# Ranking twelve batches of tokens one stage earlier in a fused attention and mixture-of-experts kernel

## What is computed

```
y   = LN(attention(LN(x)))            # 16 heads of 64, one shared k/v head, causal,
                                      # learned relative-position bias, one null key
out = x + shared(y) + sum over the 2 best of 7 experts of w_e * expert_e(y)
expert(h) = (silu(h @ g.T) * (h @ u.T)) @ d.T      # 128 -> 352 -> 128
w = the two best softmax(y @ wr.T + rb), scaled to sum to 1
```

## Time and profile before

| what | value |
|---|---|
| three timed runs | 437.86, 432.62, 437.17 us; median 437.17 |
| the profiled execution: its own time | 437.97 us |
| the profiled execution: span, first to last instruction | 436.2 us |
| TensorE (PE) busy | 359.3 us, 82% |
| VectorE (DVE) busy | 291.2 us, 67% |
| ScalarE (ACT) busy | 279.5 us, 64% |
| GpSimd (POOL) busy | 228.7 us, 52% |
| mean granted TensorE clock | 0.923 of full speed |

### The profile page before, as it was taken

One profiled execution on the slowest core, in us unless ns is written; L12 is line 12 of the kernel. 1 busy time (PEld: TensorE's weight loads), 2 busy tenths in 40 slices (PEclk: granted clock), 3 DMA queues, 4 the chain that ended last, 5 costly groups with the idle time before them and its releaser, 6 DMA issues. The chain is left out here.

```text
span 436.2 us, 10247 instructions
## 1 busy us (share of the span) xinstructions
PE 359.3 (82%) x2921; PEld 297.6 (68%) x2922; DVE 291.2 (67%) x1144; ACT 279.5 (64%) x935; POOL 228.7 (52%) x253
## 2 busy tenths in 40 slices
PE   0286776999999999999997989587948999999930
PEld 0275655677777777777775647487948999899920
DVE  2838385888888898888889893568524555555514
ACT  1374684999999999999996783345523444444410
POOL 5024833688766667667772542076750444444430
PEclk9997995999999999999999687859997999999995
DMA  6726199970000000000000000011111222121118
GB/s 187 198 78 198 52 221 207 207 141 2 2 2 2 3 2 2 3 0 2 2 2 2 1 2 0 2 50 51 55 43 45 57 61 61 49 60 58 39 19 271
DMA packets 39479, 26.54 MB, mean 61 GB/s; under 512 B 4465, under 2 KB 37131, under 8 KB 39439
## 3 DMA queue, kind: packets, MB, share of 16 engines
q1 hardware_dynamic: 33680, 19.55, 20.1%
q0 software_dynamic: 2240, 4.23, 2.9%
q10 hardware_dynamic: 3518, 2.26, 1.8%
HBM read 12.89 MB, written 13.54 MB: 61 GB/s over the span
## 5 line engine op out<-in xcount | busy, mean ns | idle before, releaser
L675 ACT ACTIVATE p_space<-p_space,low 128x129 f32<-128x129 f32 x256 | 99.0, 392 | 6.3 <-DVE low L1011 6.3
L494 POOL TENSOR_TENSOR p_space<-p_space,inv 128x516 f32<-128x516 f32 x64 | 67.0, 1049 | 66.1 <-DVE inv L1019 66.1
L1007 DVE SCALAR_TENSOR_TENSOR p_space<-bank,rn,biasm_space 128x129 f32<-128x129 f32 x256 | 72.1, 344 | 22.2 <-PE bank L1181 21.9
L485 POOL TENSOR_TENSOR biasm_space<-bias,madd 128x516 f32<-128x516 f32 x64 | 75.6, 1193 | 7.4 <-DVE p_space L1007 7.3
L536 POOL DMA_INDIRECT result_rows<-oT_space,dest_ring x38 | 37.3, 982 | 60.3 <-DVE dest_ring L1147 60.3
L760 ACT ACTIVATE biasm_space<-bank 128x384 f32<-128x384 f32 x54 | 26.6, 492 | 58.3 <-PE bank L1178 58.2
L1178 PE MATMUL bank<-ident,p_space 128*128 128x128 f32 (+1 forms) x272 | 48.5, 297 | 2.4 <-POOL p_space L494 2.1
L675 ACT ACTIVATION_READ_ACCUMULATOR p_space<-p_space,low 128x1 f32 x256 | 48.6, 190 | 0.0
L1181 PE MATMUL bank<-DT,biasm_space 128*128 (+1 forms) x324 | 46.5, 281 | 1.3 <-ACT biasm_space L760 1.3
L1181 PE MATMUL bank<-GH,yh 128*128 (+1 forms) x108 | 41.3, 382 | 6.8 <-DVE yl L1118 6.8
L690 ACT ACTIVATE pT<-bank 128x512 f32<-128x512 f32 x64 | 37.3, 583 | 13.7 <-PE bank L1181 12.5
(11 more groups left out here) (217 smaller groups left out, 682.8 us busy)
## 6 DMA issues: line engine op xcount, KB each, us to landing
sent_rows<-fill_row SPq DMA_DIRECT2D x2, 1950.0 KB, 23.0
sent_rows<-fill_row SPq DMA_DIRECT2D x2, 1885.0 KB, 19.1
q_space<-sent_rows SPq DMA_DIRECT2D x38, 65.0 KB
xs<-in_x_dram SPq DMA_DIRECT2D x4, 256.0 KB, 6.4
bias<-bias_rows SPq DMA_DIRECT2D x1, 1024.0 KB, 6.0
xnT<-result_rows ACTq DMA_DIRECT2D x4, 256.0 KB, 6.1
xn<-result_rows SPq DMA_DIRECT2D x4, 256.0 KB, 5.2
out_dram<-xs SPq DMA_DIRECT2D x4, 256.0 KB, 2.4
```

The lines of the kernel that those rows point to most:

```text
L485: nc.gpsimd.tensor_tensor(biasm[:, b % 2, heads, :], bias[:, heads, :], madd[:, b:b + 1, :].to_broadcast([P, HC, KEYS]), ALU.add).then_inc ...
L494: nc.gpsimd.tensor_tensor(v, v, spread(inv[:, b % 2, heads], KEYS), ALU.mult).then_inc(p_normed, 1)
L675: last = nc.scalar.activation(v, v, ACT.Exp, bias=low[:, b % 2, h:h + 1], accum_out=den[:, b % 2, h:h + 1])
L1007: last = nc.vector.scalar_tensor_tensor(Pb[:, q, h, :], src, rn[:, q, h:h + 1], biasm[:, q, h, :], ALU.mult, ALU.add)
```

## The change

- `choose(0)` is followed at once, in step 18, by `mark(0)`, `rank(0)` and `share_out(0)` on VectorE, all ahead of `keep_y` of batch 15. `count(0)` stands at the head of step 18 on TensorE, ahead of `mix(3, 3)`, and `weigh(0)` at the head of step 18 on ScalarE, ahead of `keep_oT(1, 3)`.
- `count(0)` writes into `bank[3]` instead of `bank[6]`, and waits for the copy of the transposed y that was in `bank[3]`.
- A send no longer waits for shared tiles.
- Tiles 8 to 15 are written out instead of looped. `AHEAD = 16` takes the place of `NB` in the order of tiles; the order itself stays the same.
- Both halves of the results are read by SyncE, eight DMAs, the two halves of a group one after the other. The second half goes into the space of `bias` instead of `xnT`.

```diff
+    AHEAD = 16
+    LAPS = (ROUTED - RING) // RING
...
+        shared_rows = bias[:, :, :].rearrange("p a b -> p (a b)")[:, 0:NB * D].rearrange("p (b d) -> p b d", d=D)
...
-        result_in = (xn, xnT[:, :].rearrange("p (b d) -> p b d", b=NB))
+        result_in = (xn, shared_rows)
...
+        def count_bank(k):
+            return (3, 6)[k]
...
             for u in range(2 * RING):
                 single(u)
                 between(u)
-            with eng.Fori(0, NB // RING - 2) as i:
-                for m in range(RING):
-                    step(RING * i + (2 * RING + m), m, i + 2, lambda k: "shared")
-            for u in range(NB, NB + RING):
+            for u in range(2 * RING, AHEAD + RING):
                 single(u)
...
-        def load_results(eng, k):
+        def load_results(eng):
...
             for g in range(NB // 4):
-                eng.dma_start(result_in[k][:, 4 * g:4 * g + 4, :],
...
+                for k in range(TOP):
+                    eng.dma_start(result_in[k][:, 4 * g:4 * g + 4, :],
...
                     for b in batches:
-                        need(pool, down_kept, min((TOP * batches.start + n * len(batches) + b - batches.start - 8) // 2, NB - 3))
                         nc.gpsimd.indirect_dma_start(
...
                 if t == NB + 1:
                     exp(3, 2)
+                if t == NB + 2:
+                    weigh(0)
                 keep_q(0)
                 keep_pT(0)
...
             nc.scalar.activation(send[0][1][:, :, 0:D], y_sb[:, 0:Y_FIRST, :], ACT.Copy).then_inc(send_made[0][1], 1)
-            weigh(0)
...
             run_tiles(act, step, between)
-            load_results(act, 1)
...
                 if t == NB + 2:
                     choose(0)
+                    mark(0)
+                    rank(0)
+                    share_out(0)
                 keep_y()
...
-            mark(0)
-            rank(0)
-            share_out(0)
             own(nc.vector.memset(h_sb[:, :, I:ICH * IC], 0.0))
...
+                if k == 0:
+                    pe.wait_ge(yT_kept, y_bank.index(count_bank(0)) + 1)
+                mm(bank[count_bank(k)][:, 2 * k * P:2 * k * P + n * NE], before[:, :], load_flat, True, True)
...
+                if t == NB + 2:
+                    count(0)
                 queries(0)
                 turn_p(0)
                 mix(3, 3)
...
             pe.wait_ge(oT_kept, 2 * NB)
-            count(0)
```

More of the change, by code:

```diff
@@ L296, in run_tiles, with kind_of @@
         def run_tiles(eng, step, between):
+            def kind_of(n):
+                return None if not 0 <= n < TILES else "routed" if AHEAD <= n < AHEAD + ROUTED else "shared"
             def single(u):
-                step(u, u % RING, u // RING, lambda k: None if not 0 <= u - k < TILES else
-                     "shared" if u - k < NB else "routed")
+                step(u, u % RING, u // RING, lambda k: kind_of(u - k))
             for u in range(2 * RING):
@@ L312, in run_tiles, with batch_of @@
                 for m in range(RING):
-                    step(RING * i + (NB + RING + m), m, i + (NB // RING + 1), lambda k: "routed")
-            for u in range(NB + RING + LAPS * RING, TILES + 3):
+                    step(RING * i + (AHEAD + RING + m), m, i + (AHEAD // RING + 1), lambda k: "routed")
+            for u in range(AHEAD + RING + LAPS * RING, TILES + 3):
                 single(u)
+        def batch_of(n):
+            return n if isinstance(n, int) and n < AHEAD else n - ROUTED
         def load_expert(sp, e, p):
@@ L647, in keep_yT, with weigh @@
                 nc.scalar.activation(YT[:, g * 512:(g + 1) * 512], bank[y_bank[g]][:, :], ACT.Copy).then_inc(yT_kept, 1)
+            def weigh(k):
+                b = slice(PARTS[k].start, PARTS[k].stop)
+                act.wait_ge(gap_made, k + 1)
+                nc.scalar.activation(share[:, 1, b], share[:, 3, b], ACT.Exp).then_inc(gap_exped, 1)
             def step(t, p, on):
@@ L741, in _ @@
             run_steps(act, step)
[L743 to L746, removed]
             act.wait_ge(biasm_first, 2 * NB)
@@ L963, in rank @@
                 own(nc.vector.tensor_copy(up[:, 0, pad + 1:pad + n, :], tot[:, 1:n, :]))
-                own(nc.vector.tensor_tensor(place[:, b, :], bank[6][:, 2 * k * P:2 * k * P + n * NE].rearrange("p (b e) -> p b e", b=n),
+                own(nc.vector.tensor_tensor(place[:, b, :], bank[count_bank(k)][:, 2 * k * P:2 * k * P + n * NE].rearrange("p (b e) -> p b e", b=n),
                                             totals[:, b, :], ALU.subtract))
@@ L1286, in count @@
                 load_flat = load[:, b, :].rearrange("p b e -> p (b e)")
-                mm(bank[6][:, 2 * k * P:2 * k * P + n * NE], before[:, :], load_flat, True, True)
-                mm(bank[6][:, (2 * k + 1) * P:(2 * k + 1) * P + n * NE], ones[:, :], load_flat, True, True).then_inc(ranks_made, 1)
+                if k == 0:
+                    pe.wait_ge(yT_kept, y_bank.index(count_bank(0)) + 1)
+                mm(bank[count_bank(k)][:, 2 * k * P:2 * k * P + n * NE], before[:, :], load_flat, True, True)
+                mm(bank[count_bank(k)][:, (2 * k + 1) * P:(2 * k + 1) * P + n * NE], ones[:, :], load_flat, True, True).then_inc(ranks_made, 1)
             def step(t, p, on):
@@ L1442, in step @@
             def step(u, m, lap, kind):
-                if isinstance(u, int) and u == NB:
+                if isinstance(u, int) and u == AHEAD:
                     pe.wait_ge(table_made, 1)
@@ L1446, in step @@
                 if kind(0) == "routed":
-                    r = u - NB
-                    pe.wait_ge(rows_loaded[m], 16 * (lap - NB // RING + 1))
+                    pe.wait_ge(rows_loaded[m], 16 * (lap - AHEAD // RING + 1))
                     pe.wait_ge(yl_made, u)
@@ L1472, in step @@
                     last.then_inc(down_made, 1)
-                if m == RING - 2 and kind(0) != "shared":
-                    load_experts(u - (NB + RING - 2))
+                if m == RING - 2 and kind(1) == "routed":
+                    load_experts(u - (AHEAD + RING - 2))
                 if kind(2):
```

31 lines of the change are left out of this document (15 added, 16 removed).

## The result

The changed kernel takes 433.58 us, the median of 20 runs (431.01 to 435.08); the kernel before takes 437.40 (432.62 to 438.29, 20 runs). The ratio is 0.9937, 95% interval 0.9916 to 0.9959. The gain is real, and smaller than the one predicted (5.4 us or 1.2%, to 431.8 us): some 2.8 us by the ratio, half of it, and 3.8 us by the medians. The profiled execution took 434.40 us with a span of 432.2, against 437.97 and 436.2.

The account below looks back on a forecast made before the run. The prediction took GpSimd's chain of 32 sends and whatever starts it as the bound. From 437.97 us it took 3.8 (first send), 1.2 (removed wait) and 0.4 (read-back): 432.6, or 431.8 as median, range 427.5 to 434.3.

Parts of the forecast that it names:

- What bounds the kernel, and the first send: GpSimd's send chain into the experts is the bound; an earlier count brings its first send 3.8 us forward, to 278.8.
- What waits behind: Work behind the moved count: `mix(3, 3)` 0.7 us later, `keep_y` hardly waits, shared tiles start 3.1 us earlier.
- The sends: GpSimd's 31 steps: removing the wait, seen once, saves 1.21 us, 40.76 to 39.55; last send at 318.3.
- The stall: TensorE's idle time before the first routed tile: shrinks from 6.93 to 5.1 us, that tile starting at 323.4.
- the clock behind the stall: First routed tiles: 3.31 us at half clock, 1.65 us of work lost, taken as unchanged by the shorter stall.
- the read-back: Loading results at the end: one queue as fast as two, last group of additions starts 0.4 us earlier.
- the upper bound: Read-back: the first pair, no longer sharing the engines with the rest, arrives 1.2 us earlier, at 426.6.
- Rival 5: Whole run: the new kernel's runs sit on the level of the earlier 432.62 us run, giving 427.3; chance 0.12.
- Rival 1: Routed tiles: the shorter stall keeps the clock up, giving 430.1, or 429.3 with the read-back's upper bound; chance 0.14.
- Rival 2: Read-back: one queue is slower, the last pair up to 4.3 us late, giving 434.0 to 436.5; chance 0.10.
- Rivals 3 and 4: Read-back over 5.0 us late, slower than before, chance 0.03; first send not brought forward, 435.5, chance 0.06.
- four signs of being wrong: First send moves under 3 us; send pitch rises; stall ends off the load; last additions wait for data past 427.05.

Follow-up runs that it names:

- e6: Changed kernel with tiles 8 to 15 in the hardware loop again: 433.81 us, ratio 0.9966 to the kernel before.
- a0: The changed kernel timed again, nothing altered, beside the kernel before: 433.22 us, ratio 0.9951.
- e2: Changed kernel with the second half of the results read on ScalarE's queue again, target left in `bias`: 432.96 us, ratio 0.9938 to the kernel before.
- e9: Changed kernel, eight read-back DMAs on the one queue, all of the first half before all of the second: 435.71 us, ratio 0.9998 to the kernel before.
- e1: Kernel before with only the first part's choice, count, rank, shares and exponential moved to step 18; sends still wait: 432.65 us, ratio 0.9926.
- e4: Changed kernel with the sends' wait on shared tiles put back: 434.07 us, ratio 0.9960 to the kernel before.
- e3: Changed kernel with 30 unused matmuls filling TensorE's stall before the routed tiles: 430.06 us, ratio 0.9893 to the kernel before.
- e5: Kernel before with 42 unused matmuls in its stall of 6.93 us: 435.02 us, ratio 0.9996.
- e10: Kernel before with only the sends' wait on shared tiles removed: 436.32 us, ratio 1.0006.
- e8: Kernel before with 12 unused matmuls at the head of its stall, leaving a shorter idle stretch: 437.07 us, ratio 0.9988.
- e11: Changed kernel with 30 unused matmuls in the stall and two read-back queues, both halves of a group on one queue: 432.27 us, ratio 0.9892 to the kernel before.
- e7: Changed kernel with 30 unused matmuls in the stall and two read-back queues: 430.51 us, ratio 0.9865 to the kernel before.

## Why the prediction was wrong, point by point

**What bounds the kernel, and the first send: right.** The count started at 273.25 and took 1.03 us (forecast 273.0 and 1.0), VectorE read its bank at 274.39 (274.1), the first send started at 279.06 (278.8), and from the choice to the send 3.64 us were gained of the 3.8 forecast (the send itself came 3.48 us sooner, since the choice began 0.16 later). **What waits behind:** the shared tiles began 3.0 us earlier (3.1), `keep_y` was ready to go when the shares ended. **The sends:** 39.52 us from first to last (39.55), no gap, last at 318.58 (318.3). One small thing was read wrong: the wait on shared tiles showed twice and not once, since in the kernel before the 17th send also stood 0.38 us and not 0.30 behind a shared tile. **The stall** was 4.98 us (5.1) in front of a tile at 323.58 (323.4), and it ended on the load. **Tiles written out:** nothing, as e6 shows. Of the Trainium skill's warning that VectorE may hold up GpSimd's descriptors (DMA: Bandwidth & Descriptors, SWDGE vs HWDGE vs iDMA), nothing shows: the sends of the changed kernel take 0.95 to 1.00 us after the first, among other neighbours than before.

**The step that failed first: "the clock behind the stall", left at its old cost.** I read that the clock would still fall, and it did, but I took the half clock behind the stall as a constant. I had read it as 3.31 us; to the clock's return it was 3.49 before. After the change it was 5.05 us in the profiled execution, and 2.87 to 4.91 us in the four unfilled traces a0, e2, e6 and e9 of the changed kernel's sends. That is +0.69 us between the two traces. Over the traces, three stalls near 7 us (before, e1, e4) left 92.4 to 92.7 us for the routed tiles; the five of the changed kernel's sends left 92.3 to 93.3, mean 93.0. So I put the term at about +0.45 us on average. e3 and e5 show that the difference is clock and nothing else.

The two traces also show what my step left out, the rest of the low stretch. In both the clock stayed down for 6.8 us in all, from 3.6 us into the idle time before and from 3.2 us into it after. Of these 6.8 us the old stall of 6.93 us covered 3.3, the new one of 4.98 us only 1.8, and the rest fell on the routed tiles. The granted clock came back after the same 6.8 us in a0, e1, e4, e6, e9 and e10 too; in these eight traces stalls of 5.0 to 5.95 us left 4.6 to 5.05 us of half clock, and stalls of 6.4 to 7.1 us left 3.1 to 3.9. In e2 and e8 the low stretch was 3.4 us, and a stall of 4.6 or 4.9 us left 2.9 or 3.4. When the fall comes and which of the two lengths follows stays open. The Trainium skill (TensorE: Matmul & The Clock Gate, Part 1: The HAM clock gate) says that the monitor's activity window runs free of the kernel, so that one kernel sees different warm-ups from run to run. The first trace of the changed kernel and a0 agree with that: the fall came 3.2 us after TensorE went idle in one and 3.8 in the other.

**The step that failed second: the read-back.** Forecast -0.4, measured +0.16 between the two traces and +0.6 over all (13.1 against 12.5). The first addition did come 0.5 us sooner after the last send, 6.32 instead of 6.85, less than half of the 1.2 that the upper bound had named. I had taken it that the last data sets the end and that one queue brings it as early as two. Instead the second pair came late (0.88 us of waiting here, and the first two groups 2.2 to 2.9 us apart in the five traces), and with it everything after. The last data came later too: the eighth transfer landed 11.2 us after the last result's send, and 11.4 to 12.4 in the other four traces, against 10.7 before. Of the Trainium skill's rule that DMAs of all issuers share the same engines and a second issuer saves issue time only (DMA: Bandwidth & Descriptors, Issuing engines are not separate DMA queues), this was to leave the sum as it stood. For the last landing e9 agrees, 10.9 us on one queue against 10.6 to 10.9 on two; what the rule does not cover is when particular transfers land, and the additions wait for those. So the pairs cost on one queue (12.7 to 13.9 us to the last addition) and on two (13.74 once), and by e9 the single queue as such costs next to nothing. Why a queue brings alternating halves later is not shown.

**A third share: the level of the run.** Rival 5 took the run of 432.62 us for a level of its own. The traces show where a large part of it comes from: in e2, e3, e4, e5 and e10 the clock is full over the choice. This is the window of e10, and the kernel before had 0.52 in the same one:

```profile
270.00:274.00 4.00, 2.74 (x22) 2.35 (x20) 1.72 (x11) 2.77 (x5) 0.00 (x0) 1.00 0.00 0
```

In the full-clock traces the choice itself begins 2.2 to 2.7 us sooner than in the two traces of the result, and the choice-to-send stretch is 12.0 us with the old order (e5, e10) and 9.1 with the new (e2, e3, e4), a gain of 2.9 instead of 3.6 to 4.0, and the removed wait is worth 0.6 instead of 1.2. The prediction worked both terms from one execution at half clock. By the traces the sends' gain is then 4.9 us in one sort of run and 3.5 in the other. Half way between them, minus 0.45 for the clock, 0.6 for the read-back and 0.4 outside the span, that is 2.7 us, beside 2.8 by the ratio of all runs and 3.8 by the medians. This is an estimate: how many runs were of each sort is not counted.

**A term put at nothing: the time outside the span.** The forecast started from the profiled execution's own time and took off only what happens inside its span. The 0.4 us that the changed kernel needs outside it are missing from the sum.

**The rivals.** Rival 1 was wrong: the clock fell in every trace with an unfilled stall, and the cost behind the stall rose on average. Rival 2 (one queue is slower, by up to 4.7 us over the forecast) was right in direction only: the read-back came out 0.6 us over the forecast between the two traces and 1.0 over all, and by e9 the order is the cause. Rivals 3 and 4 did not happen, and the median did not sit on rival 5's level. Of the four signs of being wrong that the prediction named none came: the last group of additions began at 428.13, later than 427.05, but without a wait for its data. The list had no sign for a longer half clock.

## What to carry to other kernels

Where a stall is shortened, price the clock behind it again, with its spread: what the stall no longer covers of the low clock falls on the work, and may give back part of the gain. If the stall can't be removed, try some unused matmuls in it, here worth 2.2 to 2.4 us (30 of them, e3) and 1.8 us (42, e5). A transfer split in parts is paid at the part that is needed next, so look at when each part lands and not only at the last. And measure a term in executions of both clock levels before it is added up, since what is saved of a chain of small operations depends on the level.

## What the runs showed of the hardware

- TensorE at half clock lost half of the time it spent there: 3.49 us cost 1.77 (e5), 4.7 to 5.05 us cost 2.2 to 2.4 (e3 against a0 and the first trace).
- The granted clock fell between 2.75 us (e10) and 5.05 us (e8) after TensorE went idle, in e8 0.15 us after it had started again. It then stayed at half for 6.8 us in eight of the ten traces with an unfilled or partly filled stall and for 3.4 us in two (e2, e8).
- Four 256 KB transfers on each of two queues served VectorE's additions of pairs best with each pair split over the queues (12.42 to 12.55 us in seven traces); both halves on one queue brought the first pair 1.3 us later (8.02 against 6.73 us, e11 and e7).
- An indirect send of 128 rows held its pitch of 1.26 us with and without a semaphore wait in front of it.
